# A four-layer graph network on one core: fp8 adjacency for VectorE in the attention layer, and another projection and epilogue placement in the fourth layer

## The chip, the cores and the metric

The kernel runs on one core of a Trainium2 chip. The metric is device time in microseconds (us) for one execution of the whole program. The core has a matrix engine (TensorE, PE in the profile; PEld is its weight load), VectorE (DVE), ScalarE (ACT), GpSimd (POOL) and SyncE (SP, which here only issues DMAs). Each engine runs its own instruction stream in order and waits on semaphores for the others.

## What is computed

The reference, cut to what matters. N is 3327 nodes with 256 features, and `adj` is a 0/1 matrix with about 1% ones. Padded sizes are 26 tiles of 128 nodes, or 13 pairs of tiles.

```python
h = relu(layernorm(x))
# layer 0: graph attention, positive and negative
e = leaky_relu(Wh1 + Wh2.T, 0.2); mask = adj > 0
att  =  softmax(where(mask,  e, -1e12), axis=1)
natt = -softmax(where(mask, -e, -1e12), axis=1)
x = x + elu(concat([att @ h, natt @ h], axis=1) @ wtrans)
h = relu(layernorm(x))
# layer 1: normalised adjacency
x = x + relu((D^-1/2 adj D^-1/2 @ h) @ W1 + b1)
h = relu(layernorm(x))
# layer 2: binary features and weights
x = x + relu(adj @ (binary(h) @ sign(W2).T))
h = relu(layernorm(x))
# layer 3 ("the fourth layer"): t is a scalar
s = h @ W3
x = x + (1 - t) * s + t * (adj @ s)
```

## The kernel before

Everything is one program with one hand-written instruction stream per engine, in `fast_program`. (`general_program` is a fallback for inputs outside the fast path's bounds; it does not run here.)

**Attention layer.** For each of 13 pairs of row tiles the adjacency block is cut into four chunks of 7, 6, 7 and 6 column tiles (`CHUNKS`, `NC` = 4). For a chunk, ScalarE makes `gb` = row term times column term (`products`, L969). VectorE in `produce` takes the minimum with the adjacency (`wm`, L1475), then the maximum times the adjacency (`gb`, L1476). ScalarE and VectorE split both results into f16 high and low parts of `s_mat` (L979, L985, L1481, L1486), and TensorE multiplies them by `x_mat` (L1209), with one more matmul on the fp8 adjacency `a8` for the row sums (L1212). VectorE reads the adjacency from an f32 buffer `a32`, which SP loads chunk by chunk (`load_chunk`, L734). TensorE reads `a8`, which GpSimd's DMA queue loads with a cast (`load_a8`, L880), and SP stores `a8` to `a8_dram` (L745) for the later layers. Before the first pair, the column terms go through memory: `e_rows` is stored to `e_dram` and read back broadcast as `e_tile` (L757, L738). In the first pair TensorE also computes the projected features (`weigh`, L1163), which ScalarE and VectorE split into `x_mat` (`x0_high` L956, `x0_low` L1456).

**Layers 1 to 3** are loops over 26 row tiles. Each tile is 26 matmuls ("blocks") of a 128x128 fp8 adjacency block by a row of `x_layer` (L1280): 512 columns wide in layers 1 and 3, where features are f16 high and low side by side, and 256 wide in layer 2. The fp8 pairs of tiles come from `a8_dram` into `a8_pair`, an alias of `a32`. Blocks of tile t carry the *epilogue* of tile t-1 in between, at the block numbers of `EPILOGUE_AT`: part 0 turns the result (two transposes, L1193), part 1 multiplies it by the layer's 256x256 weight (`project`, L1199, f32). In layer 3, VectorE's `product` combines the two halves of the accumulated sum with `x_layer` in three chained instructions (L1635, L1637, L1639, after ScalarE's L1077). They end in the semaphore `z_done[3]`, for which part 0 waits. ScalarE copies the turned block (`turned_copy`, L1091), TensorE projects, VectorE adds the residual (`update`, L1671) and SP stores it. After that VectorE checks a half row of the raw adjacency for values other than 0 and 1 (`check`, L1621). A tile also waits at its start for `z_done[layer]` of the tile two before, since there are two accumulators, `bank_a[0]` and `bank_a[1]`.

In layers 1 and 3 the epilogue of tile 0 stands alone between tiles 1 and 2. In layer 1, VectorE makes its range checks (L1718 to L1726, "flags") once, between the epilogue work of tile 0 and that of tile 1; `update(1)` (L1646 to L1658) ends in `binary_done`, for which TensorE waits in tile 3 before `sign_turn` (L1263).

```python
EPILOGUE_AT = {1: (9, 15), 3: (13, 19)}
...
pe.wait_ge(z_done[layer], t - 1)
...
v.tensor_tensor(part(wm, c), part(gb, c), part(a32, c), ALU.min).then_inc(wm_done, 1)
```

## Time and profile before

| | |
|---|---|
| time, median of 3 runs | 1020.51 us (1019.0 to 1021.59) |
| profiled execution, its own time | 1019.47 us |
| its span in the profile | 1017.8 us |
| busy: PE, PEld, DVE, ACT, POOL | 980.7, 723.5, 761.8, 456.8, 76.3 us |
| mean granted TensorE clock | 0.981 of full speed |

The span ends with the last instruction or DMA; 1.67 us of the execution's time lie outside it. In timelines each line gives start, duration, engine, source line, operation, tiles, and how many instructions were merged. A bracket gives the idle time before and the instruction that ended it. Matmuls overlap, so their cadence is read from starts and not from their durations.

### The profile page before, as it was taken

Reading aid. Unit: us, or ns where it says so; the run is one execution under the profiler, and the core shown is the slowest. Engines: PE = TensorE matmul, PEld = TensorE weight load, DVE = VectorE, ACT = ScalarE, POOL = GpSimd, SP = SyncE. Lnnn points to the kernel's source line nnn. Section 1 sums busy time; section 2 is a strip of 40 time slices with the busy share of each in tenths; the row PEclk is TensorE's granted clock in tenths of the full one; section 3 lists DMA queues with packets and bytes.
Section 4 is the critical chain, followed back from the end, with each engine's and each line's share of the span. In section 5 each row is a group of like instructions: output and inputs, shape, how many; then the busy total and the mean of one; then the engine's idle time right before and its main releaser. Section 6 shows DMA issues by size and latency. Waiting matters only on the chain.

```text
span 1017.8 us, 21222 instructions
## 1 busy us (share of the span) xinstructions
PE 980.7 (96%) x7701; PEld 723.5 (71%) x7701; DVE 761.8 (75%) x1141; ACT 456.8 (45%) x821; POOL 76.3 (7%) x156
## 2 busy tenths in 40 slices
PE   8979999999999999999998799999999998999996
PEld 8747788888888888888885255555568874555553
DVE  6687889999999999999997566555557775555553
ACT  5475777677777667777767322222220001111111
POOL 3000000000000000000030000000003320000000
PEclk9989999999999999999999699999999999999998
DMA  6144566676676667767553135554654446666662
GB/s 235 20 77 97 118 141 154 151 161 149 126 164 130 152 149 160 147 127 166 124 149 135 34 134 187 182 187 157 223 180 158 137 166 205 206 204 203 209 220 61
DMA packets 44045, 154.82 MB, mean 152 GB/s; under 512 B 5068, under 2 KB 25189, under 8 KB 43877
## 3 DMA queue, kind: packets, MB, share of 16 engines
q1 hardware_dynamic: 35285, 142.37, 40.6%
q0 software_dynamic: 7488, 11.08, 14.1%
q10 hardware_dynamic: 1232, 0.85, 0.3%
q8 instruction: 23, 0.38, 0.2%
q14 instruction: 17, 0.14, 0.0%
HBM read 173.02 MB, written 14.50 MB: 184 GB/s over the span
## 4 chain that ended last, share of the span: by engine, by line
PE 48%; DVE 28%; issue 12%; ACT 8%; DMA 2%; DVEq 1%; ACTq 0%; POOL 0%; POOLq 0%
PE f_ya L1280 34%; DVE f_wm L1475 9%; DVE f_gb L1476 6%; DVE f_s_mat L1481 6%; PE f_yb L1199 5%; ACT f_gb L969 4%; ACT f_s_mat L979 2%; PE f_yb L1171 1%; PE f_ya L1163 1%; PE f_ya L1209 1%; PE f_yb L1209 1%; PE f_yb L1193 1%; DVE f_s_mat L1486 1%; PE f_yb L1163 1%; DVE f_xs L1516 1%
## 5 line engine op out<-in xcount | busy, mean ns | idle before, releaser
L1209 PE MATMUL f_ya<-f_x_mat,f_s_mat 128*128 128x257 f16 x2028 | 350.7, 272 | 1.9 <-DVE f_x_mat L1456 1.9
L1209 PE MATMUL f_yb<-f_x_mat,f_s_mat 128*128 128x257 f16 x2028 | 332.3, 273 | 0.0
L1280 PE MATMUL f_ya<-f_x_mat,f_a 128*128 128x512 f16 x1352 | 323.3, 384 | 9.2 <-DVE f_x_mat L1544 9.2
L1280 PEld LDWEIGHTS f_ya<-f_x_mat,f_a 128*128 128x128 fp8e4 x1352 | 132.0, 98 | 149.3 <-DVE f_x_mat L1544 16.7
L1209 PEld LDWEIGHTS f_yb<-f_x_mat,f_s_mat 128*128 128x128 f16 x2028 | 195.4, 96 | 27.1
L1209 PEld LDWEIGHTS f_ya<-f_x_mat,f_s_mat 128*128 128x128 f16 x2028 | 149.9, 97 | 19.3 <-issue 2.6
L969 ACT ACTIVATE f_gb<-f_e_tile,f_expc 128x256 f32<-128x256 f32 x338 | 140.0, 497 | 1.9 <-issue 1.9
L979 ACT ACTIVATE f_s_mat<-f_wm 128x1792 f16<-128x1792 f32 (+1 forms) x52 | 82.8, 1592 | 115.2 <-DVE f_wm L1475 109.7
L1212 PE MATMUL f_ya<-f_ones,f_a 128*128 128x1 f16 x676 | 112.9, 167 | 0.0
L1475 DVE TENSOR_TENSOR f_wm<-f_gb,f_a 128x1792 f32<-128x1792 f32 (+1 forms) x52 | 98.2, 1889 | 18.7 <-ACT f_gb L969 16.9
L1621 DVE SCALAR_TENSOR_TENSOR f_gb<-f_gb 128x1664 f32<-128x1664 f32 x52 | 98.1, 1887 | 11.9 <-DVE f_s_mat L1671 11.9
L1481 DVE SCALAR_TENSOR_TENSOR f_s_mat<-f_wm,f_s_mat 128x1792 f16<-128x1792 f32 (+1 forms) x52 | 98.4, 1892 | 6.1 <-ACT f_s_mat L979 2.7
L1476 DVE SCALAR_TENSOR_TENSOR f_gb<-f_gb,f_a 128x1792 f32<-128x1792 f32 (+1 forms) x52 | 98.1, 1887 | 0.0
L1486 DVE SCALAR_TENSOR_TENSOR f_s_mat<-f_gb,f_s_mat 128x1792 f16<-128x1792 f32 (+1 forms) x52 | 98.0, 1886 | 0.0
L985 ACT ACTIVATE f_s_mat<-f_gb 128x1792 f16<-128x1792 f32 (+1 forms) x52 | 82.8, 1592 | 7.7 <-DVE f_gb L1476 6.1
L1077 ACT ACTIVATE f_s_mat<-f_ya,f_t_scaled 128x256 f32<-128x256 f32 x26 | 12.3, 474 | 159.2 <-PE f_ya L1280 159.2
L1280 PE MATMUL f_ya<-f_s_mat,f_a 128*128 128x256 f16 x676 | 74.9, 273 | 1.0 <-ACT f_s_mat L1086 0.6
L1280 PEld LDWEIGHTS f_ya<-f_s_mat,f_a 128*128 128x128 fp8e4 x676 | 65.9, 98 | 9.4 <-ACT f_s_mat L1086 0.8
L1212 PEld LDWEIGHTS f_ya<-f_ones,f_a 128*128 128x128 fp8e4 x676 | 66.1, 98 | 8.5
L880 POOL DMA_DIRECT2D f_a<-adj_t_dram x52 | 28.3, 545 | 462.3 <-PE f_yb L1209 441.5
L1077 ACT ACTIVATE f_s_mat<-f_ya,f_root 128x256 f32<-128x256 f32 x26 | 12.3, 474 | 103.7 <-PE f_ya L1280 103.7
L1199 PE MATMUL f_yb<-f_s_mat,f_yt_sb 128*128 128x256 f32 x208 | 55.4, 390 | 1.6 <-ACT f_yt_sb L1091 1.6
(144 smaller groups left out, 732.9 us busy)
## 6 DMA issues: line engine op xcount, KB each, us to landing
f_gb<-adj_dram SPq DMA_DIRECT2D x52, 832.0 KB, 5.0
f_a<-f_a_dram SPq DMA_DIRECT2D x39, 832.0 KB, 4.5
f_a<-adj_t_dram SPq DMA_DIRECT2D x26, 896.0 KB, 6.6
f_a<-adj_t_dram SPq DMA_DIRECT2D x26, 768.0 KB, 6.2
f_a<-adj_t_dram POOLq DMA_DIRECT2D x26, 224.0 KB, 4.9
f_a_dram<-f_a SPq DMA_DIRECT2D x26, 224.0 KB, 6.6
f_a<-adj_t_dram POOLq DMA_DIRECT2D x26, 192.0 KB, 4.6
f_a_dram<-f_a SPq DMA_DIRECT2D x26, 192.0 KB, 6.1
```

The costliest lines, as they stand in the source:

```text
L969: made = a.activation(blocks(gb, c)[:, j - lo, :], e_tile[:, r, :], ACT.Copy, scale=expc[:, 0, j:j + 1])
L979: a.activation(weights(c, 2), blocks(wm, c), ACT.Copy, scale=DOWN).then_inc(hm_done, 1)
L985: a.activation(weights(c, 0), blocks(gb, c), ACT.Copy, scale=UP).then_inc(hp_done, 1)
L1199: mm = pe.matmul(bank[:, 0:F], yt_sb[:, c * P:(c + 1) * P], w[:, c, :], start=(c == 0), stop=(c == blocks - 1))
L1209: return pe.matmul(bank[:, 0:F + 1], s_mat[:, j, side, i], x_mat[:, j, x_side, 0:F + 1], start=start, stop=stop)
L1212: pe.matmul(ya[s, p][:, F + 1:F + 2], a8[:, j, i], ones16[:, 0:1], start=False, stop=(j == TILES - 1), skip_group_check=True)
L1280: return pe.matmul(bank_a[p][:, 0:W], a8_pair[:, r, at:at + P], x_layer[layer][:, j, 0:W], start=(j == 0), stop=(j == TILES - 1))
L1475: v.tensor_tensor(part(wm, c), part(gb, c), part(a32, c), ALU.min).then_inc(wm_done, 1)
L1476: v.scalar_tensor_tensor(part(gb, c), part(gb, c), 1.0, part(a32, c), ALU.max, ALU.mult).then_inc(wp_done, 1)
L1481: v.scalar_tensor_tensor(weights(c, 3), blocks(wm, c), DOWN, weights(c, 2), ALU.mult, ALU.subtract)\
L1486: v.scalar_tensor_tensor(weights(c, 1), blocks(gb, c), UP, weights(c, 0), ALU.mult, ALU.subtract)\
L1621: v.scalar_tensor_tensor(gb[:, half, 0:HW], gb[:, half, 0:HW], 0.0, gb[:, half, 0:HW], ALU.is_gt, ALU.not_equal, accum_out=bad[:, bass.ds( ...
```

## The change

It has five parts.

1. VectorE reads the adjacency of the attention layer from `a8` in fp8. `a32` and its 52 loads are gone; `a8` holds two pairs and also serves as `a8_pair`. GpSimd's first eight loads wait for nothing now, and the others wait for TensorE and VectorE to be done with the pair two before, and for its store.
2. Layer 3's projection multiplies f16 high and low halves: the turned block is split by ScalarE (`zt16[:, 0]`) and VectorE (`low3`, new), the weight is split once (`w3_16`), and six f16 matmuls replace two f32 ones. `update` rescales.
3. In layer 3 the epilogue moves from blocks 13 and 19 to blocks 9 and 17, and the epilogue of tile 0 moves into tile 2 (the third tile) at blocks 8 and 14, with that of tile 1 at 17 and 22 (`LATE_AT`).
4. VectorE gets nine more instructions in its flags part of layer 1: range checks of the layer-3 weight and of t, and the low half of the split weight.
5. The order of the two `a8_pair` slots is reversed, and SP's waits before the layers follow the new buffers.

```diff
-        EPILOGUE_AT = {1: (9, 15), 3: (13, 19)}
+        EPILOGUE_AT = {1: (9, 15), 3: (9, 17)}
+        LATE_AT = (8, 14, 17, 22)
...
                 def load_a8(m, c):
 
                     lo, hi = CHUNKS[c]
-                    if not isinstance(m, int) or m > 0:
-                        g.wait_ge(s_free, NC * m + c - NC + 1)
+                    if m > 1:
+                        g.wait_ge(s_free, NC * (m - 2) + c + 1)
                         g.sem_inc(waited, 1)
-                        g.wait_ge(a8_stored[c], 16 * m)
+                        g.wait_ge(wp_done, NC * (m - 2) + c + 1)
                         g.sem_inc(waited, 1)
...
-                g.wait_ge(et_done, 2)
                 for m in range(PAIRS):
...
+                a.wait_ge(late_w, 64)
+                a.activation(w3_16[:, 0], w_sb[3], ACT.Copy, scale=WT).then_inc(w3_done, 1)
...
-                            a.activation(yt_sb[:, 0:F], ep[:, 0:F], ACT.Copy).then_inc(zt_done[layer], 1)
+                        if layer == 3:
+                            a.activation(zt16[:, 0], ep[:, 0:F], ACT.Copy, scale=Z3).then_inc(zt_hi, 1)
...
+                        pe.wait_ge(zt_done[3], t + 1)
+                        for c in range(FB):
+                            for half, w_half in ((0, 0), (0, 1), (1, 0)):
+                                mm = pe.matmul(op[:, 0:F], zt16[:, half, c * P:(c + 1) * P], w3_16[:, w_half, c, :],
+                                               start=(c + half + w_half == 0), stop=(c == FB - 1 and half == 1))
...
-                    v.wait_ge(a_here[c % 2], 16 * (2 * m + c // 2 + 1))
+                    v.wait_ge(a8_here[r, c], 16 * k + 16)
...
-                    v.tensor_tensor(part(wm, c), part(gb, c), part(a32, c), ALU.min).then_inc(wm_done, 1)
-                    v.scalar_tensor_tensor(part(gb, c), part(gb, c), 1.0, part(a32, c), ALU.max, ALU.mult).then_inc(wp_done, 1)
+                    v.tensor_tensor(part(wm, c), part(gb, c), a8_part(r, c), ALU.min).then_inc(wm_done, 1)
+                    v.scalar_tensor_tensor(part(gb, c), part(gb, c), 1.0, a8_part(r, c), ALU.max, ALU.mult).then_inc(wp_done, 1)
...
+                    def low3(t):
+
+                        v.wait_ge(zt_hi, t + 1)
+                        v.scalar_tensor_tensor(zt16[:, 1], ep[:, 0:F], Z3, zt16[:, 0], ALU.mult, ALU.subtract)\
+                         .then_inc(zt_done[3], 1)
...
                             if layer == 3:
-                                product(t, p)
-                            if not (first and p == 0):
-
-                                update(t - 1, 1 - p, k if p else k - 1, first)
+                                low3(t)
```

TensorE, the loop over the tiles of layer 3, one tile and a half, before:

```order
L1280 MATMUL f_ya<-f_x_mat,f_a 128x512 x13
L1193 MATMUL f_yb<-f_ident,f_y_sb 128x128 x2
L1280 MATMUL f_ya<-f_x_mat,f_a 128x512 x6
L1199 MATMUL f_yb<-f_s_mat,f_yt_sb 128x256 x2
L1280 MATMUL f_ya<-f_x_mat,f_a 128x512 x20
```

And in the changed kernel (L1293 is the block, L1196 the transposes, L1269 the projection):

```order
L1293 MATMUL f_ya<-f_x_mat,f_a 128x512 x9
L1196 MATMUL f_yb<-f_ident,f_y_sb 128x128 x2
L1293 MATMUL f_ya<-f_x_mat,f_a 128x512 x8
L1269 MATMUL f_yb<-f_s_mat,f_yt_sb 128x256 x6
L1293 MATMUL f_ya<-f_x_mat,f_a 128x512 x18
```

The transposes of a tile's result stand four blocks earlier, the projection two blocks earlier and as six matmuls.

VectorE in layer 1, the end of the flags part and the start of `update(1)`, in the changed kernel (before, the row with L1757, there L1726, was followed by the row with L1667, there L1646):

```order
L1757 TENSOR_REDUCE f_flags<-f_w_far 128x1
L1758 TENSOR_REDUCE f_w_top<-f_s_mat 128x2
L1759 TENSOR_REDUCE f_w_top<-f_s_mat 128x2
L1760 SCALAR_TENSOR_TENSOR f_w_top<-f_w_top 128x2
L1762 TENSOR_SCALAR f_w_far<-f_w_top 128x2
L1763 SCALAR_TENSOR_TENSOR f_w_far<-f_w_top,f_w_far 128x2
L1765 TENSOR_REDUCE f_flags<-f_w_far 128x1
L1766 TENSOR_TENSOR f_w_top<-f_t_col 128x1
L1767 TENSOR_SCALAR f_flags<-f_w_top 128x1
L1769 SCALAR_TENSOR_TENSOR f_s_mat<-f_s_mat 128x512
L1770 UNCONDITIONAL_BRANCH
L1770 ISA
```

Nine instructions, L1758 to L1769, now stand between the old flags and `update(1)`.

## Rows read from the trace of the kernel before

**Rows 1.** Windows: busy time per engine (x instructions), granted clock, DMA share, GB/s.

```profile
350.00:400.00 50.00, 50.00 (x514) 44.42 (x512) 45.96 (x46) 35.17 (x56) 3.24 (x6) 1.00 0.67 152
900.00:950.00 50.00, 50.00 (x241) 26.70 (x240) 28.37 (x46) 6.39 (x15) 0.00 (x0) 1.00 0.65 222
```

**Rows 2.** Page, costliest groups: busy us, mean ns of one, idle before.

```profile
L1475 DVE TENSOR_TENSOR f_wm<-f_gb,f_a 128x1792 f32<-128x1792 f32 (+1 forms) x52 | 98.2, 1889 | 18.7 <-ACT f_gb L969 16.9
...
L1481 DVE SCALAR_TENSOR_TENSOR f_s_mat<-f_wm,f_s_mat 128x1792 f16<-128x1792 f32 (+1 forms) x52 | 98.4, 1892 | 6.1 <-ACT f_s_mat L979 2.7
```

**Rows 3.** Timeline of TensorE, one tile of layer 3.

```profile
896.92 4.48 PE L1280 MATMUL f_ya<-f_x_mat,f_a 128*128 128x512 f16 x20
901.24 0.38 PE L1193 MATMUL f_yb<-f_ident,f_y_sb 128*128 128x128 f32 x2
...
902.75 1.03 PE L1199 MATMUL f_yb<-f_s_mat,f_yt_sb 128*128 128x256 f32 x4
903.62 4.48 PE L1280 MATMUL f_ya<-f_x_mat,f_a 128*128 128x512 f16 x20
```

**Rows 4.** Timeline of ScalarE, the same tile.

```profile
901.66 0.38 ACT L1091 ACTIVATE f_yt_sb<-f_yb 128x256 f32<-128x256 f32 x1 [2.55 <-PE f_yb L1193]
```

**Rows 5.** Timeline of VectorE, the same tile.

```profile
899.22 0.48 DVE L1635 SCALAR_TENSOR_TENSOR f_y_sb<-f_ya,f_t_scaled,f_s_mat 128x256 f32<-128x256 f32 x1 [2.24 <-ACT f_s_mat L1077]
...
900.50 0.48 DVE L1639 SCALAR_TENSOR_TENSOR f_y_sb<-f_x_mat,f_omt_scaled,f_y_sb 128x256 f32<-128x256 f32 x1
```

**Rows 6.** Timeline of TensorE, start of layer 3, tile 0's epilogue alone.

```profile
842.95 0.44 PE L1193 MATMUL f_yb<-f_ident,f_y_sb 128*128 128x128 f32 x2 [2.00 <-DVE f_y_sb L1639]
843.95 1.10 PE L1199 MATMUL f_yb<-f_s_mat,f_yt_sb 128*128 128x256 f32 x4 [0.56 <-ACT f_yt_sb L1091]
844.89 2.97 PE L1280 MATMUL f_ya<-f_x_mat,f_a 128*128 128x512 f16 x13
```

**Rows 7.** Timeline of VectorE, start of layer 3, the third instruction of product(0).

```profile
842.41 0.48 DVE L1639 SCALAR_TENSOR_TENSOR f_y_sb<-f_x_mat,f_omt_scaled,f_y_sb 128x256 f32<-128x256 f16 x1
```

**Rows 8.** Timeline of VectorE, the flags part of layer 1 and what follows.

```profile
586.59 1.22 DVE L1722 TENSOR_REDUCE f_w_top<-f_wtrans_sb 128x4 f32<-128x1024 f32 x1
587.85 0.16 DVE L1723 SCALAR_TENSOR_TENSOR f_w_top<-f_w_top 128x4 f32<-128x4 f32 x1
...
588.63 0.42 DVE L1646 TENSOR_TENSOR f_w_res<-f_yb,f_s_mat 128x256 f32<-128x256 f32 x1
```

**Rows 9.** Groups of instructions by line, VectorE's split of another weight.

```profile
L1385 DVE SCALAR_TENSOR_TENSOR f_y_sb<-f_wtrans_sb,f_y_sb 128x512 f16<-128x512 f32 x2 | 1.3, 689 | 1.5 <-ACT f_y_sb L938 1.5
```

**Rows 10.** Timeline of TensorE, layer 1, and the attention layer's first pair.

```profile
590.98 0.29 PE L1263 MATMUL f_ya<-f_s_mat 128*128 128x128 f16 x2 [0.57 <-DVE f_s_mat L1658]
...
61.08 2.74 PE L1163 MATMUL f_yb<-f_y_sb,f_x_mat 128*128 128x512 f16 x6 [5.47 <-DVE f_x_mat L1456]
...
575.48 1.88 PE L1280 MATMUL f_ya<-f_x_mat,f_a 128*128 128x512 f16 x4 [3.61 <-DVE f_x_mat L1544]
```

**Rows 11.** Windows of 1 us, columns as in the first group.

```profile
60.00:61.00 1.00, 0.00 (x0) 0.00 (x0) 1.00 (x4) 1.00 (x2) 0.00 (x0) 0.56 0.00 0
...
66.00:67.00 1.00, 1.00 (x4) 0.31 (x3) 1.00 (x1) 0.59 (x2) 0.00 (x0) 0.53 0.00 0
...
842.00:843.00 1.00, 0.05 (x1) 0.05 (x1) 0.96 (x3) 0.00 (x0) 0.00 (x0) 1.00 0.80 206
```

**Rows 12.** Timeline of ScalarE, the wait for e_tile in the first pair.

```profile
53.24 2.90 ACT L969 ACTIVATE f_gb<-f_e_tile,f_expc 128x256 f32<-128x256 f32 x7 [1.94 <-issue]
```

**Rows 13.** Timeline of GpSimd, its first loads of a8.

```profile
23.65 0.20 POOL L870 TENSOR_TENSOR f_nmr<-f_neg_mean,f_root 128x6 f32<-128x6 f32 x1
44.57 2.39 POOL L880 DMA_DIRECT2D f_a<-adj_t_dram  x4 [20.73 <-ACT f_e_rows L950]
```

**Rows 14.** Timeline of VectorE, the first pair, its last instruction before TensorE's first weighted block.

```profile
65.22 2.02 DVE L1486 SCALAR_TENSOR_TENSOR f_s_mat<-f_gb,f_s_mat 128x1792 f16<-128x1792 f32 x1
```

**Rows 15.** Page, DMA queues: packets, MB, share of 16 engines over the span.

```profile
q0 software_dynamic: 7488, 11.08, 14.1%
```

145 lines of the change are left out of this document (87 added, 58 removed).

## The prediction, made before the changed kernel ran

> **What bounds the kernel now.** I read the windows by stage first, then the timelines of the places that the diff touches. In the attention layer and in layer 3 TensorE has no idle time at full clock, while VectorE is busy 46 of 50 us and 28 of 50 us [rows 1]. So in both a change pays or costs only through TensorE's own work or through a wait put in front of it. The page's groups give the price of VectorE's big instructions [rows 2]. The tile of layer 3 is then read on three engines [rows 3 to 5]; the reader is to see there when the result of a tile is ready for the transposes. Its start, where tile 0's epilogue stands alone, is the next place [rows 6, 7]. The flags part of layer 1 and the short wait behind it follow [rows 8 to 10], then the places where the clock falls [rows 11], and at last the beginning of the attention layer [rows 12 to 15]. Terms are in us against the profiled execution's 1019.47, which is 1.04 below the median of the three runs.
>
> **Layer 3, tiles 3 to 25: the saving.** Blocks come every 0.216 (20 from 896.92 to 901.24) and the transposes take 0.22. The f32 projection takes 0.87, from 902.75 to 903.62 [rows 3]. A tile is the time from one 20-block row to the next, 6.70. Six f16 matmuls of 256 columns are half as wide as a block, so 6 x 0.108 = 0.65. The saving is 0.22 a tile.
>
> **The same tiles: the wait.** The tile begins seven blocks after 896.92, at 898.43 [rows 3]. VectorE's three chained instructions follow ScalarE's from 899.22, and the third ends at 900.50 + 0.48 = 900.98 [rows 5]. That is 2.55 after the tile's beginning. The seven-block offset is there because the 20 merged blocks are the last seven of one tile and the first thirteen of the next. Block 13 comes at 13 x 0.216 = 2.81, so today the transposes never wait. Block 9 comes at 9 x 0.216 = 1.94. In the changed kernel TensorE reaches the transposes with 0.61 to go, plus 0.06 from VectorE's end to the transposes behind it (842.41 + 0.48 to 842.95 [rows 6, 7]). So each tile waits 0.67. TensorE runs in order and has nothing else: the wait is paid in full, and nothing behind it can absorb it, since the chain begins at the end of the previous tile. The net is 0.67 - 0.22 = +0.45 for each of 23 tiles, **+10.4**. The bounds are +10.1 (the chain has a gap of 0.16 before the second and the third instruction [rows 5]; in the last tiles, which are written out behind the loop, it may not be there) and +11.5 (0.05 a tile to refill the array, the difference of 0.44 and 0.38 for the pair of transposes after a wait and without one [rows 3, 6]).
>
> Does the new `low3` add another wait? After the transposes ScalarE starts 0.42 later and needs 0.38 [rows 3, 4]. `low3` reads the accumulator like L1635, so 0.48, plus some 0.15 of handover [rows 5]. It ends 1.43 after the transposes begin, while block 17 comes 0.22 + 8 x 0.216 = 1.95 after them. There is 0.5 of cover, so it costs nothing. On VectorE's own queue only `update`'s one short instruction stands between, done before ScalarE's copy. `low3` holds up only the check behind it, and VectorE has over 20 of 50 us free [rows 1].
>
> **Layer 3, the first tiles.** The move of tile 0's epilogue into tile 2 should fill the 2.00 and the 0.56 of idle [rows 6]. But tile 2 writes the accumulator of tile 0 and waits for its `z_done`, the very signal that ends the 2.00. So only the 0.56 and the projection leave this place. Tile 2 begins at 842.95 instead of 844.89. Its transposes at block 8 come at 844.68. ScalarE's stream has `turned_copy(0)` ahead of `product(1)`, so it copies until 845.5 and hands over tile 1's half at about 845.85. VectorE's stream has `product(1)` ahead of `low3(0)`: four times 0.5 later, with the handover at 847.95, `low3(0)` ends. TensorE wanted it at block 14, at 846.19, and waits 1.8. At block 22 `low3(1)` stands behind a 1.9 check and `update(0)`, another 0.4. Tile 2 would end at 842.95 + 5.62 of blocks + 0.43 of transposes + 1.30 of projections + 2.2 of waits = 852.5. Today it ends at 844.89 + 6.70 = 851.6. **+0.9**, with bounds of -1.3 (neither wait) and +1.5.
>
> **Layer 1, VectorE's nine new instructions.** `update(1)` starts at 588.63 with no idle before it, right behind the flags [rows 8], and TensorE already waits 0.57 for its result [rows 10]. So all nine stand on the path. A 1024-element reduction takes 1.26 to the next start [rows 8]; at one element a cycle half of it leaves about 0.71, twice 1.42. Six small ones at 0.2 give 1.2 (L1723 is of that kind [rows 8]). The split of the weight is as L1385, 0.69 [rows 9], 0.6 of it before the next one starts. The sum is **+3.2**. The wait of TensorE grows to 3.8. It idles 3.61 before 575.48 and behind it four blocks take 1.88, so the clock is at the half, 1.2 GHz [rows 10]. After 2.00 of idle, at 842, it stays at 1.00 [rows 6, 11]. A wait of 3.8 is nearest to the first. At the half, in the first pair, the stretch from 61.08 to 67 lasted 5.9 us and did half the work, a loss of 2.9 [rows 10, 11]. I take **+2.4**, between 0 (no fall) and 2.9. Later tiles of the layer have slack on VectorE and don't give it back or lose more.
>
> **Attention layer, steady state.** The two instructions that read fp8 are not in the trace with that type. The nearest rows are f32 with f32 at 1889 ns and f32 with f16 at 1892 ns [rows 2]: the second operand's width makes no difference. I take 0. VectorE could bear 4 us in 50 more; only above that does it cost anything. The Trainium skill, VectorE: DVE Perf Modes, Side-by-side table, gives the base mode for everything and the faster ones only where the data are 16 bits wide or there is one source; by it an fp8 operand beside an f32 one changes nothing either, and the sum stays. No row here has the fp8 operand. The 52 loads that go had no waiter: TensorE doesn't idle here [rows 1].
>
> **Attention layer, the beginning.** ScalarE is ready for the first `products` at 51.30 and starts at 53.24, after 1.94 of wait for `e_tile` [rows 12], whose load ran beside GpSimd's four cast loads from 44.57 [rows 13]. Those and four more now start at about 24, behind the last `nmr` at 23.65 [rows 13]. The queue's share, 14.1% of 1017.8 over 13 pairs, is 11.0 for four loads [rows 15]. Eight are done near 46 and `e_tile` should come in time: -1.9 on everything until TensorE. There the idle of 5.47 becomes 3.5 [rows 10]. It is in the 5.47 that the clock falls, at 60 to 61, and the half lasts until 67 [rows 11], worth up to 2.9 more. TensorE has 24 matmuls from 61.08 before the first weighted block, some 8 us as the clock went (6 took 2.74 [rows 10]), and VectorE has the weights ready at 67.2 [rows 14]; that leaves about 2.1 of the 2.9. The bounds are 0 (the loads still collide) and -4.0; 3.5 of idle is like the 3.61 that fell, while here the fall came 4.9 after the idle began. I take **-2.9**, the middle. Nothing else changes there.
>
> **The end.** `low3(25)` adds 0.6 behind ScalarE, and the last projection at the half clock is shorter by about as much: 0. The SP queue loses work, its loads for layer 1 start when TensorE ends the attention layer and have 25 us and more to land: 0.
>
> **Sum.** 10.4 + 0.9 + 3.2 + 2.4 - 2.9 = +14.0, so 1033.5 on the profiled execution, 1034.5 on the median. I say 1034.
>
> **The rivals.**
> *The transposes don't wait* (the other side). Decides if `product` ends less than 1.94 after the tile begins; rows 5 say 2.55 in every tile I looked at, and nothing in the change shortens the chain. Then layer 3 gives 23 x -0.22 = -5.1 instead of +10.4: 1018 to 1019, and with both clocks lucky (-1.0 and -2.4) 1015, faster than before. Chance 6%.
> *No fall of the clock in layer 1, none in the first pair.* -2.4 and -1.1: 1031. Both the other way, with `e_tile` still late: 1038. These are inside the forecast.
> *fp8 reads at half the speed.* VectorE's two instructions a chunk would go from 1.9 to 3.8, four chunks a pair: +15 a pair against 2.5 of room, 12 pairs: +150, 1170. Nothing in rows 2 speaks for it. 3%.
> *The clock oscillates in layer 3.* TensorE would now stop 0.67 in every 7.15. Against it: idle of 2.00 and 0.56 within 4 us left the clock at 1.00 [rows 6, 11]. If it fell, tiles would take up to 5.6 more, +130: 1160. 2%. The Trainium skill, TensorE: Matmul & The Clock Gate, A second HAM failure mode, describes a kernel whose small idles between groups of matmuls made the clock swing between its two levels; by that rule this rival would hold, and so far the trace disagrees.
> *The change's gain elsewhere is bigger than I see* (an unseen wait goes), or a new one comes: 4%.
>
> **How the numbers follow.** The forecast has 85%. Its terms at their good ends give 10.1 - 1.3 + 3.2 + 0 - 4.0 = 8.0, at their bad ones 11.5 + 1.5 + 3.4 + 2.9 + 0 = 19.3, so 1028 to 1040 on the median's footing; not all will go one way. The range of 1027 to 1040 leaves out the rivals and a little of the forecast. About 0.3% is what a measurement can tell here. Faster than 1017.4: half of the first rival and some of the unseen, 5%. Within 0.3%: 5%. Slower: 90%.
>
> **What would show it.** In the changed kernel's trace, a tile of layer 3 should take 7.15, with the transposes idle some 0.67 before them, waiting for VectorE's L1660. The projection should show six matmuls in 0.65 with no idle. Tile 2 should show a wait of 1.8 at its first projection. TensorE in layer 1 should wait 3.8 before `sign_turn`, and the clock there should show the half. ScalarE should start the first L969 with no wait, at 51.3. VectorE's fp8 instructions should last 1.89. I am wrong if tiles of layer 3 take 6.5.

## The result: slower by 1.1%, as forecast, with two terms of the sum off

| | before | after |
|---|---|---|
| median | 1020.03 us (4 runs, 1019.0 to 1021.59) | 1031.73 us (4 runs, 1029.09 to 1036.11) |
| profiled execution, its own time | 1019.47 us | 1036.11 us |
| its span | 1017.8 us | 1034.2 us |
| mean granted TensorE clock in it | 0.981 | 0.978 |

The ratio is 1.0112, with a 95% interval of 1.008 to 1.0144. The forecast was 1034 us, with a range of 1027 to 1040. The profiled execution of the changed kernel is the slowest of its four, 4.4 us over their median. So its trace shows more than the median pays; the section on the prediction says what the 4.4 are.

**The loop of layer 3.** TensorE's timeline, one period and the start of the next (start us, us, engine, line, operation, count, idle before and what ended it):

```profile
858.52 0.44 PE L1196 MATMUL f_yb<-f_ident,f_y_sb 128*128 128x128 f32 x2 [0.51 <-DVE f_y_sb L1660]
858.79 1.89 PE L1293 MATMUL f_ya<-f_x_mat,f_a 128*128 128x512 f16 x8
860.52 0.82 PE L1269 MATMUL f_yb<-f_s_mat,f_yt_sb 128*128 128x256 f16 x6
861.17 4.05 PE L1293 MATMUL f_ya<-f_x_mat,f_a 128*128 128x512 f16 x18
865.75 0.44 PE L1196 MATMUL f_yb<-f_ident,f_y_sb 128*128 128x128 f32 x2 [0.52 <-DVE f_y_sb L1660]
```

The period is 865.75 - 858.52 = 7.23 us against 6.69 before [rows 3]. The projection takes 861.17 - 860.52 = 0.65 and waits for nothing. The 18 blocks that begin at 861.17 are issued by 861.17 + 18 x 0.216 = 865.06, and the transposes start 0.69 later. The bracket shows only 0.52, because the last block still drains and counts as busy. VectorE's timeline says what they wait for, in the same tile:

```profile
864.57 0.48 DVE L1658 SCALAR_TENSOR_TENSOR f_y_sb<-f_x_mat,f_omt_scaled,f_y_sb 128x256 f32<-128x256 f32 x1 [0.18 <-DVE f_y_sb L1656]
865.20 0.48 DVE L1660 SCALAR_TENSOR_TENSOR f_y_sb<-f_x_mat,f_omt_scaled,f_y_sb 128x256 f32<-128x256 f32 x1
```

The third instruction ends at 865.68, and the transposes follow at 865.75. The waits of TensorE, added up over the trace, put this one first (engine, line, what it waited for: us in total, times, longest):

```profile
PE f_yb L1196 <- DVE f_y_sb L1660: 14.0, 24, 2.2
...
PE f_ya L1276 <- DVE f_s_mat L1679: 4.8, 2, 3.4
PE f_yb L1166 <- DVE f_x_mat L1477: 3.4, 1, 3.4
PE f_yb L1269 <- DVE f_yt_sb L1699: 2.5, 2, 1.6
```

Of the 14.0 us, the longest wait of 2.2 stands behind the last tile and was there before the change too. The rest belongs to the loop.

In the window of 50 us that stands in [rows 1], TensorE is no longer busy throughout, yet the clock stays at 1.00 (columns as in [rows 1]):

```profile
900.00:950.00 50.00, 46.33 (x237) 22.81 (x236) 28.13 (x49) 5.54 (x13) 0.00 (x0) 1.00 0.56 189
```

**The start of layer 3.** TensorE's timeline, to be read beside [rows 6]:

```profile
845.00 3.56 PE L1293 MATMUL f_ya<-f_x_mat,f_a 128*128 128x512 f16 x8 [2.04 <-issue]
848.37 0.41 PE L1196 MATMUL f_yb<-f_ident,f_y_sb 128*128 128x128 f32 x2
848.61 1.46 PE L1293 MATMUL f_ya<-f_x_mat,f_a 128*128 128x512 f16 x6
851.67 0.81 PE L1269 MATMUL f_yb<-f_s_mat,f_yt_sb 128*128 128x256 f16 x6 [1.60 <-DVE f_yt_sb L1699]
```

The idle of 2.04 ahead of tile 2 is where the prediction has it. The wait of 1.60 us (1.8 with the drain) ahead of the first projection is too. New is that the eight blocks from 845.00 take 3.37 us instead of 1.73: the granted clock fell to the half.

**Layer 1.** VectorE's flags part, whose nine new instructions begin at 584.95, then TensorE's wait for what stands behind them:

```profile
584.95 0.68 DVE L1758 TENSOR_REDUCE f_w_top<-f_s_mat 128x2 f32<-128x512 f32 x1
...
587.30 0.68 DVE L1769 SCALAR_TENSOR_TENSOR f_s_mat<-f_s_mat 128x512 f16<-128x512 f32 x1
587.90 0.41 DVE L1667 TENSOR_TENSOR f_w_res<-f_yb,f_s_mat 128x256 f32<-128x256 f32 x1
```

```profile
590.23 0.40 PE L1276 MATMUL f_ya<-f_s_mat 128*128 128x128 f16 x2 [3.39 <-DVE f_s_mat L1679]
590.42 1.91 PE L1293 MATMUL f_ya<-f_x_mat,f_a 128*128 128x512 f16 x4
```

The nine take 587.90 - 584.95 = 2.95 us. The wait went from 0.57 [rows 10] to 3.39. Behind it four blocks take 1.71 to the next start instead of 0.86: the half clock again.

**The attention layer's beginning.** ScalarE, GpSimd and TensorE, to be read beside [rows 12], [rows 13] and [rows 10]:

```profile
51.25 2.89 ACT L966 ACTIVATE f_gb<-f_e_tile,f_expc 128x256 f32<-128x256 f32 x7
...
24.21 4.73 POOL L878 DMA_DIRECT2D f_a<-adj_t_dram  x8 [0.33 <-issue]
...
59.07 1.93 PE L1166 MATMUL f_yb<-f_y_sb,f_x_mat 128*128 128x512 f16 x6 [3.41 <-DVE f_x_mat L1477]
```

ScalarE's wait for `e_tile` is gone and TensorE's idle went from 5.47 to 3.41. The six matmuls behind the idle start 2.0 us earlier. The 24 matmuls from there to the first weighted block take 6.87 us instead of 8.07, since less of the stretch lies at the half clock. So the first weighted block starts at 65.94 instead of 69.15. The reads of fp8 cost what the f32 reads did, 1887 and 1886 ns in the mean over 52 each, against 1889 [rows 2].

**Where the 16.4 us of span went.** The beginning -3.2, a shorter drain into layer 1 -0.4, layer 1 +5.6 (2.8 of wait and 2.7 of clock), the start of layer 3 +2.3 (1.6 of it the clock), the loop +11.8 and its last tile +0.3, the end 0.0: together +16.4.

### The profile page after: what moved, and what is told of

The parts are those of the page before. It is cut to its first block, busy times and chain, and to the rows that moved or that the text cites. A ratio compares the mean times of both kernels' runs of the same rounds, so it can differ in the third digit from the quotient of the medians.

```text
span 1034.2 us, 21206 instructions
## 1 busy us (share of the span) xinstructions
PE 982.9 (95%) x7753; PEld 717.7 (69%) x7753; DVE 771.8 (75%) x1176; ACT 456.8 (44%) x822; POOL 76.5 (7%) x156
## 3 DMA queue, kind: packets, MB, share of 16 engines
q0 software_dynamic: 7488, 11.08, 13.6%
## 4 chain that ended last, share of the span: by engine, by line
PE 76%; DVE 12%; issue 6%; ACT 4%; DMA 1%; DVEq 1%; POOL 0%; ACTq 0%; POOLq 0%
PE f_ya L1293 30%; PE f_ya L1212 18%; PE f_yb L1212 17%; PE f_yb L1202 2%; DVE f_wm L1496 2%; PE f_yb L1269 2%; PE f_yb L1196 2%; PE f_ya L1166 2%; DVE f_gb L1497 2%; PE f_yb L1174 1%; PE f_yb L1166 1%; DVE f_s_mat L1502 1%; ACT f_s_mat L1077 1%; DVE f_y_sb L1658 1%; DVE f_y_sb L1656 1%
## 5 line engine op out<-in xcount | busy, mean ns | idle before, releaser
L1293 PE MATMUL f_ya<-f_x_mat,f_a 128*128 128x512 f16 x1352 | 327.5, 388 | 11.0 <-DVE f_x_mat L1565 8.9
L1293 PEld LDWEIGHTS f_ya<-f_x_mat,f_a 128*128 128x128 fp8e4 x1352 | 132.8, 99 | 150.2 <-DVE f_x_mat L1565 16.1
L1496 DVE TENSOR_TENSOR f_wm<-f_gb,f_a 128x1792 f32<-128x1792 f32 (+1 forms) x52 | 98.1, 1887 | 16.6 <-ACT f_gb L966 14.8
L1497 DVE SCALAR_TENSOR_TENSOR f_gb<-f_gb,f_a 128x1792 f32<-128x1792 f32 (+1 forms) x52 | 98.1, 1886 | 0.0
L1293 PE MATMUL f_ya<-f_s_mat,f_a 128*128 128x256 f16 x676 | 74.9, 273 | 1.0 <-ACT f_s_mat L1086 0.6
L1293 PEld LDWEIGHTS f_ya<-f_s_mat,f_a 128*128 128x128 fp8e4 x676 | 65.9, 98 | 9.5 <-ACT f_s_mat L1086 0.9
L1656 DVE SCALAR_TENSOR_TENSOR f_y_sb<-f_ya,f_t_scaled,f_s_mat 128x256 f32<-128x256 f32 x26 | 12.6, 483 | 60.9 <-ACT f_s_mat L1077 60.9
```

Of the source, the lines that this page charges most:

```text
L1293: return pe.matmul(bank_a[p][:, 0:W], a8_pair[:, r, at:at + P], x_layer[layer][:, j, 0:W], start=(j == 0), stop=(j == TILES - 1))
L1496: v.tensor_tensor(part(wm, c), part(gb, c), a8_part(r, c), ALU.min).then_inc(wm_done, 1)
L1497: v.scalar_tensor_tensor(part(gb, c), part(gb, c), 1.0, a8_part(r, c), ALU.max, ALU.mult).then_inc(wp_done, 1)
```

## Experiments

All were timed against the kernel before, whose median was 1019.74 us in experiments 1 to 4, 1019.70 in 5 to 8 and 1020.71 in 9 to 12. So between these groups the ratios compare better than the medians. Ratios carry their 95% intervals. The line numbers of the diffs' surroundings are those of the changed kernel.

**1. The attention part alone.** The change without its layer 3 and without the nine instructions. A part of the diff against the changed kernel:

```diff
-        EPILOGUE_AT = {1: (9, 15), 3: (9, 17)}
+        EPILOGUE_AT = {1: (9, 15), 3: (13, 19)}
-                    apart_pairs = 2 if layer == 3 else 0
+                    apart_pairs = 0
...
-                            v.scalar_tensor_tensor(xo[:, p, :], o, 1.0 / (WT * Z3), xt, ALU.mult, ALU.add).then_inc(upd[3], 1)
+                            v.tensor_tensor(xo[:, p, :], o, xt, ALU.add).then_inc(upd[3], 1)
```

> The kernel after with its fourth layer put back as it was before: the projection in f32, the first epilogue alone ahead of the third tile, the transposes at block 13 and the projection at block 19, and the range check of the fourth layer's weights gone. What is left of the change is the attention layer with the fp8 adjacency read by VectorE and the loads' new order. My theory: all of the gain sits in the attention's start, where the wait for e_tile goes: the first exponentials of ScalarE start at 51.3 us of the span without a wait, the first weighted block 3.2 us earlier than before, layer 1 starts 3.2 to 3.6 us earlier, and nothing else moves: 1020.0 - 3.4 = 1016.6 us, ratio 0.9967. The two VectorE instructions that read fp8 stay at 1.89 us. Rival 1: the gain of the start is lost in the steady attention layer (TensorE waits for loads of a buffer of two pairs): 1020. Rival 2: the start's gain is a different clock fall and not a wait: then the gap before the first block stays at 5.5 us.

Measured: 1016.84 us against 1019.74, ratio 0.9971 (0.9956 to 0.9985). So the attention part is worth 2.9 us, near the theory's 3.4. Neither rival holds: the gain is there, and TensorE's idle ahead of the six matmuls is 3.42 in the trace, with no wait of ScalarE for `e_tile`. The ten runs range from 1014.56 to 1020.04.

**2. The epilogue back at 13 and 19.**

```diff
-        EPILOGUE_AT = {1: (9, 15), 3: (9, 17)}
+        EPILOGUE_AT = {1: (9, 15), 3: (13, 19)}
```

> The kernel after, with one pair of numbers back as before: in layer 3 the four transposes stand ahead of block 13 again and the projection ahead of block 19. My theory: all of the loop's loss is the wait of the transposes for the last of VectorE's three instructions of the product (0.67 us of each tile, of a period of 7.23), since the chain to it ends 2.55 us into the tile and block 13 comes at 2.8. So the period falls to 26 x 0.216 + 0.22 + 0.65 = 6.5 us, 22 to 23 tiles give back 0.72 each, 16 to 17 us in all: 1031.7 - 16.5 = 1015 us, and TensorE is no longer shown to wait at its transposes. The projection at block 19 (1.1 us behind the end of the transposes) may wait 0 to 0.2 for the low halves. Rival: the period is longer because of the f16 halves themselves (twelve instead of four steps around the projection, the extra VectorE instruction per tile, which delays what stands behind it): then the wait only moves to the projection and the time stays above 1025.

Measured: 1014.31 us, ratio 0.9936 (0.9912 to 0.996), where 1015 was expected. The rival needed over 1025. One pair of numbers is worth 17.4 us between the medians. TensorE's timeline of the loop:

```profile
860.52 0.38 PE L1196 MATMUL f_yb<-f_ident,f_y_sb 128*128 128x128 f32 x2
860.74 1.46 PE L1293 MATMUL f_ya<-f_x_mat,f_a 128*128 128x512 f16 x6
862.04 0.82 PE L1269 MATMUL f_yb<-f_s_mat,f_yt_sb 128*128 128x256 f16 x6
862.69 4.48 PE L1293 MATMUL f_ya<-f_x_mat,f_a 128*128 128x512 f16 x20
867.01 0.38 PE L1196 MATMUL f_yb<-f_ident,f_y_sb 128*128 128x128 f32 x2
```

The period is 6.49 and no bracket is left: the low halves arrive in time for the projection at block 19. So the f16 halves are faster than f32 by 0.21 a tile, and the earlier block costs 0.74. This run also shows layer 1 with the same wait as the profiled run of after and no fall of the clock:

```profile
589.99 0.28 PE L1276 MATMUL f_ya<-f_s_mat 128*128 128x128 f16 x2 [3.40 <-DVE f_s_mat L1679]
590.11 1.03 PE L1293 MATMUL f_ya<-f_x_mat,f_a 128*128 128x512 f16 x4
```

And it prices the start of layer 3 without a fall: from TensorE's last block of tile 1 to the end of tile 2 it takes 11.4 us, against 10.8 before, +0.6.

**3. Without eight of the nine instructions.** It leaves out the range checks of the layer-3 weight and of t; the low half of the weight stays.

```diff
-                        flag_step(v.tensor_reduce(w0_top[:, 0, 0:FB], w_sb[3], AX.X, ALU.max))
...
-                        v.tensor_scalar(flags[:, 6:7], w0_top[:, 0, 0:1], T_MAX ** 2, None, ALU.is_gt).then_inc(flc, 1)
-                                v.wait_ge(flc, 8)
-                                v.tensor_reduce(flags[:, 7:8], flags[:, 0:7], AX.X, ALU.add).then_inc(flagd, 1)
+                                v.wait_ge(flc, 6)
+                                v.tensor_reduce(flags[:, 7:8], flags[:, 0:5], AX.X, ALU.add).then_inc(flagd, 1)
```

> The kernel after without eight of the nine VectorE instructions that the change adds ahead of layer 1's loop (the range check of the fourth layer's weights and of t; this part of the computation is left out; the low half of the weights stays). My theory: they are on the path, since TensorE waits at its first sign_turn for what stands behind them: the wait of 3.39 us shrinks by the eight's 2.5 us to 0.8, and the clock doesn't fall behind it, which is worth another 2.4: 1031.7 - 4.9 = 1026.8 us. Rival 1: only the wait goes and the clock falls all the same: 1029.2. Rival 2: the wait is not caused by these instructions but by a chain beside them (the update and its statistics): then TensorE still waits 3 us there and the time stays at 1031.

Measured: 1029.59 us, ratio 1.0081 (1.0057 to 1.0105), 2.1 below the changed kernel by the medians and 3.2 by the ratios, whose intervals overlap. That is nearer to the number of rival 1 (1029.2) than to that of my theory (1026.8), but the mechanism is neither's. In the trace the wait at the second `sign_turn` is gone altogether, but at the first one the clock is at the half:

```profile
579.72 0.39 PE L1276 MATMUL f_ya<-f_s_mat 128*128 128x128 f16 x2 [1.40 <-DVE f_s_mat L1679]
579.91 1.91 PE L1293 MATMUL f_ya<-f_x_mat,f_a 128*128 128x512 f16 x4
...
588.13 0.28 PE L1276 MATMUL f_ya<-f_s_mat 128*128 128x128 f16 x2
```

So no clock falls behind a wait here: it was at the half before and rose at 582.6. The same two rows, TensorE's first and second `sign_turn`, can be read in every trace. The stretch between them is where the nine instructions stand:

| kernel | clock at the first `sign_turn` | wait at the second, us | from the first to the second, us |
|---|---|---|---|
| before; experiments 1 and 4 | full in all | 0.57 in all | 7.77; 7.78; 7.77 |
| after; experiment 2 (nine in place) | full; full | 3.39; 3.40 | 10.59; 10.60 |
| experiments 5, 6, 11 (nine in place) | half | 2.02; 1.29; 0.86 | 10.58; 10.59; 10.59 |
| experiments 3 (eight away) and 9 (nine away) | half | none | 8.41; 8.41 |
| experiments 7 and 8 (nine away) | half | none | 9.11; 9.60 |
| experiments 10 and 12 (nine away, eight fills ahead) | half | none | 8.83; 8.89 |

With the nine in place VectorE sets the length, 10.59 whatever the clock does, and a TensorE at half clock only waits less. Without them TensorE sets it and pays for its own half clock. So the nine cost 2.8 where the clock is full and 1.0 to 2.2 where it is at the half. There VectorE's work had been hiding TensorE's slowness.

**4. The kernel before with 9 and 17.**

```diff
-        EPILOGUE_AT = {1: (9, 15), 3: (13, 19)}
+        EPILOGUE_AT = {1: (9, 15), 3: (9, 17)}
```

> The kernel before with one pair of numbers of the change: in layer 3 the transposes ahead of block 9 and the projection, still in f32, ahead of block 17. My theory: the wait has nothing to do with f16: the transposes wait 0.67 us in each of 24 to 25 tiles, the period goes from 6.69 to 7.36 us, and the time from 1020.0 to 1036 (+16, ratio 1.016), 4 to 5 us more than the whole change gives. Rival: the wait of 0.67 comes with the halves (the VectorE instruction for the low half stands between a product and the next): then here the transposes wait less than 0.3 us and the time stays below 1028.

Measured: 1036.55 us, ratio 1.0155 (1.0131 to 1.0179), expected 1036. In its trace the period is 7.35 us (853.98 - 846.63), with 0.49 of idle shown at the transposes. So the wait has nothing to do with f16. With experiment 2 it gives all four corners: f32 at 13/19 (with the attention part) 1016.8, f16 at 13/19 1014.3, f16 at 9/17 1031.7, f32 at 9/17 (without the attention part) 1036.6.

**5. The epilogue at 11 and 17, a dose between the two.**

```diff
-        EPILOGUE_AT = {1: (9, 15), 3: (9, 17)}
+        EPILOGUE_AT = {1: (9, 15), 3: (11, 17)}
```

> The kernel after with the transposes of layer 3 ahead of block 11 (not 9 as in the change, not 13 as before) and the projection ahead of block 17. A dose between the two: with the transposes at block 9 TensorE waited 0.69 us, the period was 7.23 us; at block 13 there was no wait and the period was 6.485. My theory (the transposes wait for the last instruction of the product, which ends at a fixed 2.63 us of the tile): at block 11, reached at 2.38 us, 0.26 us of wait are left, and 0.05 for the start of a stopped pipe: period 6.8 us, 23 tiles x 0.31 = 7 us over the 1014.3 of block 13: 1021.5 us. Rival: the loss at block 9 comes from something that the early transposes do to the engines behind them (the low half's VectorE instruction pushed ahead of other work): then it is all or nothing, 1014 or 1031.

Measured: 1022.01 us, ratio 1.0029 (1.0016 to 1.0042), expected 1021.5. TensorE's timeline:

```profile
854.81 0.44 PE L1196 MATMUL f_yb<-f_ident,f_y_sb 128*128 128x128 f32 x2
855.08 1.46 PE L1293 MATMUL f_ya<-f_x_mat,f_a 128*128 128x512 f16 x6
856.38 0.82 PE L1269 MATMUL f_yb<-f_s_mat,f_yt_sb 128*128 128x256 f16 x6
857.03 4.48 PE L1293 MATMUL f_ya<-f_x_mat,f_a 128*128 128x512 f16 x20
861.61 0.44 PE L1196 MATMUL f_yb<-f_ident,f_y_sb 128*128 128x128 f32 x2
```

The period is 6.80. There is no bracket here and yet a wait: 857.03 + 20 x 0.216 = 861.35, and the transposes start 0.26 later, most of it hidden in the drain of the last block. Only the longer 0.44 of the pair (0.38 without a wait) tells of it. The three doses, 9, 11 and 13, fit a result that is ready 2.63 us into the tile: block 9 comes at 1.94 and waits 0.69, block 11 at 2.38 and waits 0.26, block 13 at 2.81 and waits for nothing.

**6. Both products first.** ScalarE's order at the start of layer 3, on top of 13 and 19:

```diff
+                            if layer == 3 and first:
+                                if p == 1:
+                                    product(1, 1)
+                                    turned_copy(0)
+                                else:
+                                    product(0, 0)
+                                continue
```

> The kernel with the epilogue at 13 and 19 (1014.3 us), and at the start of layer 3 ScalarE does the second tile's product ahead of the first tile's turned copy. It tells apart what the wait of 1.60 us ahead of the first f16 projection stands on. My theory: on ScalarE's order. ScalarE waits with the turned copy for the transposes in tile 2, the second product waits behind it, VectorE idles 3.09 us for that product and does the low half only behind it. With the products first VectorE does its second product at once, the low half is ready 1.0 us behind the transposes, and the projection waits 0 to 0.1: 1014.3 - 1.6 = 1012.7 us, ratio to before 0.992. Rival: VectorE's own row of work (three instructions of 0.5 us and the low half) is the chain: then the projection still waits over a microsecond, and the time stays at 1014.3.

Measured: 1014.16 us (six runs, 1011.01 to 1015.83), ratio 0.994 (0.9921 to 0.9958), against 1014.31. The projection's wait stood on ScalarE's order, as expected, but the gain is not to be seen in the median. In the trace the projection waits no longer, but the clock fell at this place:

```profile
841.40 2.53 PE L1300 MATMUL f_ya<-f_x_mat,f_a 128*128 128x512 f16 x8 [2.04 <-issue]
843.72 0.63 PE L1203 MATMUL f_yb<-f_ident,f_y_sb 128*128 128x128 f32 x2
844.14 2.34 PE L1300 MATMUL f_ya<-f_x_mat,f_a 128*128 128x512 f16 x6
846.32 0.82 PE L1276 MATMUL f_yb<-f_s_mat,f_yt_sb 128*128 128x256 f16 x6
```

**7. The nine instructions at the start of layer 3.** On top of 13 and 19, the block of nine moves in VectorE's code:

```diff
                     else:
                         check(CHECKS1, 1)
                         check(CHECKS1 + 1, 0)
+                        flag_step(v.tensor_reduce(w0_top[:, 0, 0:FB], w_sb[3], AX.X, ALU.max))
...
+                        v.scalar_tensor_tensor(w3_16[:, 1], w_sb[3], WT, w3_16[:, 0], ALU.mult, ALU.subtract).then_inc(w3_done, 1)
                         pair(0, True)
```

> The kernel with the epilogue at 13 and 19 (1014.3 us), and the change's nine VectorE instructions (range check and low half of the fourth layer's weights) moved from the start of layer 1 to the start of layer 3, behind two checks of the adjacency, where VectorE idles 3.65 us for ScalarE's first product. Nothing is left out. My theory: at the old place they lengthened TensorE's wait from 0.57 to 3.40 us and at the new one they are hidden: 1014.3 - 2.8 = 1011.5 us. Rival 1: at the new place they delay the first product by what the loads' checks leave of the idle time: then the gap ahead of tile 2 grows over 2.04 us by 1 to 3, and nothing is won. Rival 2: the clock falls at other gaps and eats it: 1013 to 1014.

Measured: 1013.13 us, ratio 0.9934 (0.992 to 0.9948), 1.2 below 1014.31, where my theory had 2.8; by the ratios the two are level. Rival 1 is out: the idle ahead of tile 2 in layer 3 is still 2.04. The wait at the second `sign_turn` is gone, and the tile ahead of it ran at the half clock, 9.11 us in the table above. That is 1.5 won and not 2.8. The time is that of rival 2, but no new gap of TensorE makes it. The half clock there began at 571, ahead of both `sign_turn`s, and in experiment 2 it had ended before the first of them.

**8. All three mends and 28 and 14 filling matmuls.**

```diff
+                            if j == 11:
+                                keep_busy(28)
                             pe.wait_ge(xlo, 2 * (j - 4) + 2)
...
+                        if late:
+                            keep_busy(14)
                         pe.wait_ge(z_done[layer], t - 1)
```

> All three mends together (epilogue at 13 and 19, both products first, the nine instructions at layer 3), and two gaps of TensorE filled with matmuls of ones by ones whose result nobody reads: 28 ahead of the wait of 3.41 us in the weighing of the features ahead of the attention layer (the granted clock is at half from 60 to 63.8 us behind it, in each trace so far), 14 ahead of the wait of 2.04 us of tile 2 in layer 3 (behind which the clock fell in one trace of three). My theory: the clock falls behind idle gaps of TensorE, and matmuls in the gap keep it up: 1014.3 - 1.6 - 2.8 = 1009.9 by the mends, and 2 us less by the clock: 1007.9. Rival 1: the fillers don't keep the clock (or run into the end of the gap and delay the path): 1010 or more. Rival 2: the start of the attention layer is bound by VectorE and ScalarE and not by TensorE, so that a full clock there only makes the next wait longer: 1009.5 to 1010, with the clock at full speed in the records all the same.

Measured: 1013.52 us, ratio 0.9933 (0.9919 to 0.9948). Rival 1 holds, and it was a miscount of mine: 28 matmuls are 56 entries in the profile and take 6.25 us to the next start, 0.22 for each matmul, in a gap of 3.41 us. TensorE's timeline:

```profile
55.47 6.41 PE L1183 MATMUL f_yb<-f_ones 128*128 128x128 f32 x56
61.72 1.46 PE L1175 MATMUL f_yb<-f_y_sb,f_x_mat 128*128 128x512 f16 x6
```

The six matmuls start 2.65 us later than at 59.07. They run at full clock (1.46 us where the changed kernel's profiled run had 1.93), so the first weighted block is only 1.1 late (66.90 against 65.80 in experiment 9). The 14 at layer 3 run 0.9 over the end of their gap. That the fills keep the clock up isn't shown by this alone: in experiments 6 and 7 the six matmuls took 1.47 behind the same gap without fills.

**9. The three mends without fills.** The diffs of 2, 6 and 7 together.

> The three mends together without any filling matmul: epilogue at 13 and 19, both products first at the start of layer 3, the nine instructions at layer 3. What is told apart is why the mends of layer 1 and of the start of layer 3, each tried alone on top of 13 and 19, took their wait out of the trace (3.40 us at the sign_turn, 1.60 us at the projection) and left the median almost where it was (1013.1 and 1014.2 against 1014.3). Theory 1: the waits are worth what they last, and clock falls differ from run to run and hid it: 1014.3 - 2.8 - 1.6 = 1009.9 us. Theory 2: the clock gives it back, since TensorE runs at half speed in a stretch that the mends only move (579 to 586 us in both traces, not in that of 13 and 19 alone): 1012.5 to 1013.5.

Measured: 1012.22 us (six runs, 1009.65 to 1013.35), ratio 0.9918 (0.99 to 0.9936). The median is just below theory 2 (the clock gives back) and its best two runs, 1009.65 and 1009.82, are at theory 1's 1009.9. By the ratios it is 1.8 below experiment 2, of the 4.4 of theory 1, and the two intervals overlap. So in some executions the waits seem to be worth what they last, and in most about half of it is not to be had. The trace is that of one of the two best. The stretch in layer 1 takes 8.41 in it, so 2.2 of its 2.8 are won.

**10. The three mends with fills that fit.**

```diff
-                                keep_busy(28)
+                                keep_busy(14)
-                            keep_busy(14)
+                            keep_busy(7)
+                    if layer == 1:
+                        for _ in range(8):
+                            pe.matmul(ep[:, 0:P], ones[:], ones[:], start=True, stop=True)
                     pe.wait_ge(x_ready[layer], TILES)
```

> The three mends, and filling matmuls that fit into their gaps (one took 0.229 us where I had counted 0.11, so 28 and 14 of them ran 2.7 and 0.9 us over the end of their gaps): 14 in the gap of 3.41 us ahead of the attention layer, 7 in that of 2.04 us of layer 3, and 8 new ones at the start of layer 1, in the gap of 3.7 to 5.2 us ahead of its last blocks, behind which TensorE ran at half speed until 586 us in three traces of five. Theory: the clock falls behind idle gaps, and a filled gap keeps it. At the attention layer that brings at most 0.5 (with a full clock TensorE was seen to wait 1.17 us for VectorE there), at layer 1 2 to 4 us (blocks of 0.43 instead of 0.22 us from 572 on), at layer 3 0 to 1.7: 3 to 5 us below the three mends alone, and a narrow spread. Rival: the clock in layer 1 falls for the whole sparse stretch from 552 us on (TensorE waits there between single blocks) and eight matmuls don't keep it: less than 1 us.

Measured: 1010.1 us (five runs, 1008.57 to 1010.73), ratio 0.9895 (0.9877 to 0.9913), the lowest median here, 1% below the kernel before. It is 2.1 below experiment 9, less than the 3 to 5 expected, and the two intervals overlap. The eight at layer 1 did not do what they were for. The granted clock of 575 to 600 us is 0.85 here and 0.86 in experiment 9. At the attention's beginning the clock stays up and VectorE takes over the bound. The first weighted block starts at 65.76, where it starts at 65.80 in experiment 9, so nothing is won there:

```profile
65.76 0.27 PE L1221 MATMUL f_ya<-f_x_mat,f_s_mat 128*128 128x257 f16 x1 [1.17 <-DVE f_s_mat L1521]
```

The spans of the two traces are the same too (1008.4 and 1008.2 us). So what the median gained lies in executions without a trace. The gap ahead of tile 2 in layer 3, where the clock falls in some of them, is a candidate; it is not shown.

**11. GpSimd's loads issued late.** On top of 13 and 19:

```diff
+                g.wait_ge(et_done, 2)
                 for m in range(PAIRS):
                     for c in range(NC):
                         load_a8(m, c)
```

> The kernel with the epilogue at 13 and 19 (1014.3 us), in which GpSimd waits again, as before the change, for the transposed exponentials before it issues its first loads of the fp8 adjacency (at 44.6 us of the span and not at 24.2). It tells apart what took the wait for e_tile away at the attention's start. The e_tile loads are issued at 45.7 us in both kernels. My theory: the gain is the loads' earlier issue: they are out of the way when e_tile is loaded. Late again, they share the DMA engines with e_tile, ScalarE's first exponentials start at 53 and not at 51.3 us, VectorE's first instruction on fp8 waits for its own load, and 2 to 4 us are lost: 1017 us. Rival: the gain is that the f32 loads of the adjacency are gone: then e_tile lands early all the same, and the time stays at 1014.3 to 1014.8.

Measured: 1017.81 us, ratio 0.9974 (0.9961 to 0.9988), 3.5 above experiment 2 by the medians and 3.9 by the ratios: the whole gain of the attention part (2.9) is gone. All of this trace stands 1.9 later from the start, so compare the waits. GpSimd, ScalarE and TensorE:

```profile
46.38 4.50 POOL L878 DMA_DIRECT2D f_a<-adj_t_dram  x8 [20.73 <-ACT f_e_rows L948]
...
55.20 2.90 ACT L967 ACTIVATE f_gb<-f_e_tile,f_expc 128x256 f32<-128x256 f32 x7 [2.08 <-issue]
...
63.02 2.74 PE L1167 MATMUL f_yb<-f_y_sb,f_x_mat 128*128 128x512 f16 x6 [5.61 <-DVE f_x_mat L1478]
```

ScalarE's wait is back (2.08, 1.94 before) and so is TensorE's idle (5.61, 5.47 before), though no f32 load of the adjacency is left. The loads of `e_tile` say the same. From issue to landing they took 8.6 us in the median before, 3.0 in the changed kernel and 8.7 here. Nor was an f32 load in their way before: SP issued two from 2.85 us and the next at 60.26. So the gain came with the removed wait of GpSimd, not with the narrower reads.

**12. The attention part with the fills.** The diff of 1, and the fills of 14 and 8 of experiment 10.

> The attention part alone (f32 projection at 13 and 19, layer 1 without the nine instructions; 1016.8 us without fills), with the fills of 14 ahead of the attention layer and 8 at the start of layer 1. Beside the kernel with three mends and fills it shows what the f16 halves of the fourth layer are worth once their side costs are gone: the period of a tile is 6.694 us in f32 and 6.485 in f16, 24 tiles x 0.21 = 5.0 us, less 0.6 at the start of layer 3. Theory: 4.5 us slower than the three mends with the same fills, and 2 to 4 us faster than the attention part alone. Rival: f16 brings less, since the clock or the low halves give it back: less than 2 us between the two.

Measured: 1017.05 us, ratio 0.9962 (0.9947 to 0.9977), where experiment 1 had 1016.84. The fills bring nothing that can be seen here, a miss for the 2 to 4 us expected. Against experiment 10 the f16 layer with its mends is 6.9 us faster, more than the 4.5 expected. The 0.21 a tile explain 5.0 of it. What the rest is, I did not separate: that kernel also has the fill and the new order of the start of layer 3, and the clock differs between executions.

## Why the prediction was right, and where it was not

- **The number: right, in part by luck.** Two terms were off in opposite directions. The loop was taken 1.7 too small, and the clock in layer 1, which the median seems not to pay (below), stood in the sum with 2.4.
- **What bounds it: right.** In layer 3 and in the attention layer TensorE had no idle time, so only its own work and waits in front of it counted. VectorE's unchanged instructions and the 52 loads that went moved nothing in the steady attention layer.
- **The loop of layer 3: right in mechanism, 1.7 us too small.** The prediction said +10.4 with bounds of 10.1 and 11.5; the trace has +12.1 with the last tile. The wait is 0.69 and not 0.67, the 0.05 a tile for the refill, which stood only in the upper bound, is paid in every tile (0.27 instead of 0.22 for the transposes), and f16 saves 0.21 and not 0.22. Experiments 2, 4 and 5 show the cause from three sides: without the early block the loss is gone, with it alone the loss is there in f32, and half the distance gives the expected part.
- **`low3` costs nothing: right.** It ends at 859.83, and the projection that reads it starts at 860.52.
- **The start of layer 3: +0.6 where the clock holds, +2.3 in the profiled run, said +0.9.** The wait at tile 2's first projection is the one predicted, and experiment 6 took it away by ScalarE's order alone. The second wait, ahead of tile 1's projection, was taken as 0.4 and is 0.1 (854.39 against the 854.27 at which the blocks before it end), which is the 0.3 between +0.9 and +0.6. The fall of the clock was not in the term: idle of 2.00 had left the clock at 1.00 [rows 6, 11], and in the profiled run of after it fell behind an idle of 2.04.
- **Layer 1, the wait: right.** 2.95 for the nine against 3.2, and a wait of 3.39 against 3.8. Experiments 3 and 7 removed it by removing or moving them.
- **Layer 1, the clock: +2.4 was right for the profiled run (2.7) and wrong as a term of the change.** In experiment 2 the clock held behind the same 3.40. The step that failed is "a wait of 3.8 is nearest to the first", the 3.61 before 575.48 [rows 10]. The row itself was read rightly: the clock was full through that idle and fell at its end, as three windows of the kernel before show below (columns as in [rows 1]). But the length of an idle did not settle what the clock did behind it. In experiment 2 it fell at the end of an idle of 3.76 (before 571.66) and held behind the 3.40, 18 us later. Without this term the runs give -2.9 + 2.8 + 0.6 + 12.1 = +12.6, against +11.7 between the medians.

```profile
571.00:572.00 1.00, 0.87 (x5) 0.20 (x2) 0.50 (x4) 0.00 (x0) 0.32 (x1) 1.00 0.00 0
574.00:575.00 1.00, 0.00 (x0) 0.00 (x0) 0.46 (x2) 0.82 (x3) 0.00 (x0) 1.00 0.00 0
576.00:577.00 1.00, 1.00 (x4) 0.18 (x2) 0.00 (x0) 0.46 (x1) 0.00 (x0) 0.50 0.00 0
```

- **The attention layer: right.** -2.9 predicted, -2.9 measured in experiment 1, -3.2 in the profiled run. Its two parts hold as well: 2.0 of earlier start for the 1.9, and 1.2 of clock for the 1.0. Experiment 11 shows the reason that the prediction gave, the earlier loads of GpSimd. The Trainium skill, VectorE: DVE Perf Modes, Side-by-side table, gives the base mode for everything and the faster ones only for 16-bit data or one source. The trace agrees, now with the fp8 operand itself: 1887 ns against 1889 [rows 2].
- **The rivals.** The transposes do wait, fp8 isn't read at half speed, and the clock doesn't swing in layer 3: 1.00 in the window of 50 us above, with a stop of 0.69 in each 7.23. The Trainium skill, TensorE: Matmul & The Clock Gate, A second HAM failure mode, describes a kernel whose clock swung with small stops between groups of matmuls. By that, tiles should have run partly at half speed; the trace disagrees for stops of this size.
- **The 4.4 us between the profiled run and the median.** Two falls of the clock, 2.7 in layer 1 and 1.6 at layer 3, make 4.3, and neither is in the trace of experiment 2, which has the same code there. That the other three executions of after lacked them I conclude from their times and their mean granted clocks, 0.982 to 0.985 against 0.978; there is no trace of them.

## What to carry to other kernels

A step that is moved earlier in an engine's row must be held against the time at which its input is ready, counted from the same mark. Here one subtraction (2.63 against 9 x 0.216) priced a loss of 17 us that hid a gain of 5 us from f16 and one of 3 us from the attention layer. A change in several parts should be taken apart before it is dropped: with the old block numbers alone it is 0.6% faster than before, with its side costs mended 0.8%, and with the fills 1%; the steps from 0.6 to 0.8 and to 1% are each within the noise. An engine that sets the pace in a stretch also hides the slowness of the others there, so a removed wait gives back only down to the next one. A wait that goes in the trace is not yet time in the median where the clock falls differ from run to run; and a fill must be counted from a measured duration.
